# Attention and convolution kernel: first period reordered, x1 passed through DRAM in another layout, keys and values moved behind the transposes

## What is computed

```python
# per sequence b: a 32x32 mixing of the tokens, whose weights come from cond
h = gelu(gelu(cond @ W0 + b0) @ W1 + b1);  att = softmax(h @ W2 + b2)
y[b] = einsum('k,koi->oi', att[b], weight) @ x[b] + (att[b] @ bias_k)[:, None]
# attention over the 32 tokens: 32 query heads, 8 key/value heads of 16, rope, causal
x1 = x + softmax(rope(y Wq) rope(y Wk).T / 4) (y Wv) @ Wo
# grouped convolution over the 512 channels (tokens are its channels): 4 groups, 9 taps
z = conv(x1) + cond @ c_weight.T + bias
# feed forward: base matrix and 8 LoRA experts, weighed by a router's softmax
out = x1 + z @ base_W.T + base_b + 2 * sum_e w_e * (z A_e.T) B_e.T
```

## Time and profile before

| | |
|---|---|
| median of 3 runs | 609.29 (609.05 to 610.1) |
| the profiled execution: its own time | 612.12 |
| the profiled execution: span of its instructions | 610.3 |
| PE busy | 586.5, 96% of the span |
| DVE / ACT / POOL busy | 494.5 / 221.4 / 225.9 |
| mean granted TensorE clock | 0.992 |

### The profile page before, as it was taken

One profiled execution on the slowest core, in us unless ns is written; L12 is line 12 of the kernel. 1 busy time (PEld: TensorE's weight loads), 2 busy tenths in 40 slices (PEclk: granted clock), 3 DMA queues, 4 the chain that ended last, 5 costly groups with the idle time before them and its releaser, 6 DMA issues.

```text
span 610.3 us, 14252 instructions
## 1 busy us (share of the span) xinstructions
PE 586.5 (96%) x4937; PEld 493.8 (81%) x4937; DVE 494.5 (81%) x1236; ACT 221.4 (36%) x603; POOL 225.9 (37%) x182
## 2 busy tenths in 40 slices
PE   5789999999999999999999999999999999999986
PEld 4577888888889888888888888888888888898864
DVE  4658788888888888888888888888888888888855
ACT  4344333333333333334333433333333334334321
POOL 7344244333333433233344333343443333334310
PEclk9879999999999999999999999999999999999999
DMA  8547553445555434455553345455534455554241
GB/s 186 109 145 158 117 130 107 94 113 112 116 133 133 116 96 111 99 112 133 133 133 109 90 111 111 113 133 133 129 101 97 107 117 117 133 133 112 64 112 59
DMA packets 122086, 71.26 MB, mean 117 GB/s; under 512 B 45661, under 2 KB 104189, under 8 KB 121944
## 3 DMA queue, kind: packets, MB, share of 16 engines
q1 hardware_dynamic: 120576, 70.53, 48.7%
q0 software_dynamic: 144, 0.28, 0.3%
q10 hardware_dynamic: 1352, 0.27, 0.2%
HBM read 51.53 MB, written 19.53 MB: 116 GB/s over the span
## 4 chain that ended last, share of the span: by engine, by line
PE 78%; DMA 10%; DVE 5%; SPq 3%; issue 2%; ACT 1%; ACTq 1%; DVEq 0%
PE ps L435 17%; PE ps L602 15%; PE ps L623 9%; DMA scratch<-x_dram 6%; PE ps L629 5%; PE ps L665 5%; PE ps L539 4%; PE ps L657 4%; PE ps L684 3%; PE ps L706 3%; PE ps L576 3%; PE ps L673 2%; PE ps L613 2%; PE ps L579 2%; DVE x1p L1290 1%
## 5 line engine op out<-in xcount | busy, mean ns | idle before, releaser
L1013 POOL TENSOR_TENSOR qk<-network,t 128x640 f32<-128x640 f32 x31 | 48.3, 1558 | 162.6 <-DVE t L1206 162.6
L435 PE MATMUL ps<-wqkv_hi,y_hi 128*128 128x512 f32 (+1 forms) x256 | 87.8, 343 | 0.9 <-POOL y_lo L1003 0.5
L435 PE MATMUL ps<-wqkv_lo,y_hi 128*128 128x512 f32 (+1 forms) x256 | 87.4, 342 | 0.0
L435 PE MATMUL ps<-wqkv_hi,y_lo 128*128 128x512 f32 (+1 forms) x256 | 87.4, 342 | 0.0
L1025 POOL TENSOR_TENSOR raw<-x1p,basebB 128x512 f32<-128x512 f32 x32 | 49.5, 1547 | 57.8 <-DVE x1p L1290 57.6
L799 ACT ACTIVATE raw<-ps 128x512 f32<-128x512 f32 x64 | 37.7, 595 | 76.0 <-PE ps L684 75.9
L1020 POOL TENSOR_TENSOR raw<-raw,zero 128x512 f32<-128x512 f32 x32 | 33.3, 1040 | 73.9 <-DVE raw L1279 73.9
L435 PEld LDWEIGHTS ps<-wqkv_hi,y_hi 128*128 128x128 f32 x256 | 48.8, 191 | 8.8 <-ACT y_hi L799 2.0
L997 POOL TENSOR_TENSOR raw<-raw,rz 128x512 f32<-128x512 f32 x32 | 33.6, 1049 | 59.4 <-DVE rz L1235 59.4
L435 PEld LDWEIGHTS ps<-wqkv_lo,y_hi 128*128 128x128 f32 x256 | 48.9, 191 | 6.1
L435 PEld LDWEIGHTS ps<-wqkv_hi,y_lo 128*128 128x128 f32 x256 | 48.8, 191 | 6.0
(11 more groups left out here) (204 smaller groups left out, 1468.9 us busy)
## 6 DMA issues: line engine op xcount, KB each, us to landing
scratch<-x_dram SPq DMA_DIRECT2D x96, 256.0 KB, 5.8
x_dram<-x1p SPq DMA_DIRECT2D x32, 260.0 KB, 2.0
xm<-x SPq DMA_DIRECT2D x32, 256.0 KB, 4.4
xr<-x SPq DMA_DIRECT2D x32, 256.0 KB, 2.7
out<-raw SPq DMA_DIRECT2D x32, 256.0 KB, 2.1
v_dram<-vS SPq DMA_DIRECT2D x32, 64.0 KB
vB<-v_dram SPq DMA_DIRECT2D x128, 16.0 KB, 4.8
mixb<-mixb_dram SPq DMA_DIRECT2D x28, 64.0 KB, 3.9
```

The source lines that it names most:

```text
L435: last = mm(dst, a, b, start=(n == 0), stop=(n == 3 * len(left) - 1))
L1013: nc.gpsimd.tensor_tensor(qk[:, :], t1, t2[:, :], ALU.add).then_inc(qk_sb, 1)
```

## The change

In the loop and the other periods:

- x1 is stored to DRAM by four DMAs (one for each phase j, each 128 runs of 520 bytes) in a layout in which each of the three xc loads is 32 runs of 8312 bytes; xc has rows of 130 columns in SBUF. All waits on `x1_out` count four DMAs.
- In t = 3 to 30 keys_values(t+1) stands behind transpose_p(t) on PE; in the others it stays.
- values' waits for vB and pT_sb become `values_ready`, which stands ahead of conv (in t = 1 behind it). The wait for `hwT_lo_sb` and the two-column product go. The hwT transpose goes to bank 3 in place of 7 (but for the last three groups).
- ACT copies both halves of the transposed probabilities before the transposed hw.

In the first period:

- SP, and not ACT, issues the loads of the mixing weights of groups 1 to 3, behind the broadcast of the bias and ahead of the store of v.
- PE runs scores(0) before it waits for these weights and mixes group 1. DVE runs the first half of softmax(0) ahead of the next y, the second half behind it.
- ACT copies v and q first, then Wo's first two parts, the exponentials' first half, and after the second half Wo's other two parts.

```diff
@@ -199,7 +199,8 @@
         oT_lo = sb("oT_lo", [P, NQ, NB, S], F32R)
         x1p = sb("x1p", [P, PH, P + 2])
         x1 = x1p[:, :, 1:P + 1]
-        xc = scratch[0:SHIFTS * S, 0:NB * PH * P].rearrange("p (q n) -> p q n", n=P)
+        xcs = scratch[0:SHIFTS * S, 0:NB * PH * (P + 2)]
+        xc = xcs.rearrange("p (q n) -> p q n", n=P + 2)[:, :, 0:P]
         z_hi = sb("z_hi", [P, PH, P], F32R)
         z_lo = sb("z_lo", [P, PH, P], F32R)
         arS = sb("arS", [P, NAR])
@@ -219,7 +220,7 @@
 
         mixb_dram = nc.dram_tensor("mixb_dram", [B, S], F32, kind="Internal").ap()
         v_dram = nc.dram_tensor("v_dram", [P, P], F32, kind="Internal").ap()
-        x1_dram = nc.dram_tensor("x1_dram", [NB * PH, CG * PH, P + 2], F32, kind="Internal").ap()
+        x1_dram = nc.dram_tensor("x1_dram", [CG * PH, NB * PH, P + 2], F32, kind="Internal").ap()
         mixw_dram = nc.dram_tensor("mixw_dram", [B, S, S], F32, kind="Internal").ap()
 
         bank = [ctx.enter_context(nc.psum_tensor(f"bank{i}", [P, 512], F32)) for i in range(0)]
@@ -300,6 +301,14 @@
         def heads(w, a):
 
             return w[:, :, :, :].rearrange("p g (b a) q -> p a g b q", a=2)[:, a, :, :, :]
+
+        def hwT_bank(u):
+
+            return 7 if isinstance(u, int) and u >= G - 3 else 3
+
+        def keys_late(t):
+
+            return not isinstance(t, int) or 3 <= t < G - 1
 
         def value_bank(a, t):
 
@@ -358,6 +367,9 @@
                     sp.dma_start(vB[S * k:S * (k + 1), :, :, at:at + HD].rearrange("m b h d -> m (b h) d"),
                                  v_dram.rearrange("(m b) (h k d) -> k m (b h) d", b=NB, h=2, d=HD)[k]).then_inc(vB_in, 16)
 
+            sp.wait_ge(mixw_zero, 1)
+            sp.wait_ge(mixw_out1, 16)
+            load_mixw(sp, 1, 4, mixw_in2)
             sp.wait_ge(pads_sb, 1)
             store_values(0)
             load_values(0)
@@ -389,10 +401,11 @@
                 if peeled(t, G - 1):
                     load_values(t)
                 if live(t - 1):
-                    sp.wait_ge(x1_out, 16 * t)
+                    sp.wait_ge(x1_out, 16 * PH * t)
+                    run = NB * PH * (P + 2) - 2
                     for s in range(SHIFTS):
-                        sp.dma_start(xc[S * s:S * (s + 1), :, :],
-                                     x1_dram[:, :, s:s + P].rearrange("q r n -> r q n")).then_inc(xc_in, 16)
+                        sp.dma_start(xcs[S * s:S * (s + 1), 0:run],
+                                     x1_dram.rearrange("r q n -> r (q n)")[:, s:s + run]).then_inc(xc_in, 16)
                 if live(t) and not peeled(t, 0) and not peeled(t, G - 1):
                     load_values(t)
                 if peeled(t, 1):
@@ -408,7 +421,8 @@
                     store_values(t + 1)
                 if live(t):
                     sp.wait_ge(x1_sb, t + 1)
-                    sp.dma_start(x1_dram.rearrange("q (i j) n -> (q i) j n", j=PH), x1p[:, :, :]).then_inc(x1_out, 16)
+                    for j in range(PH):
+                        sp.dma_start(x1_dram.rearrange("(i j) q n -> j q i n", j=PH)[j], x1p[:, j, :]).then_inc(x1_out, 16)
                 if live(t) and live(t + 1):
                     sp.dma_start(xr[:, :], group(x_g, t + 1)).then_inc(xr_in, 16)
                 if live(t + 3) and (not isinstance(t, int) or t > 0):
@@ -686,18 +700,17 @@
                     if b % 2:
                         last.then_inc(pT_ps, 1)
 
+            def values_ready(t):
+
+                pe.wait_ge(vB_in, 16 * HK * (t + 1))
+                pe.wait_ge(pT_sb, 2 * t + 2)
+
             def values(t):
 
-                pe.wait_ge(vB_in, 16 * HK * (t + 1))
-                if live(t - 2) and not peeled(t, G - 1):
-                    pe.wait_ge(hwT_lo_sb, t - 1)
                 if peeled(t, 0):
                     pe.wait_ge(prep_sb, 1)
                 if peeled(t, 1):
                     pe.wait_ge(base_lo_sb, 3)
-                pe.wait_ge(pT_sb, 2 * t + 2)
-                if not isinstance(t, int):
-                    mm(ps[0:S, 4, 0:2], convW[:, 0, :, :].rearrange("p j o -> p (j o)"), xc[:, 0, 0:2], start=True, stop=True)
                 for b in range(NB):
                     for h in range(2):
                         for r in range(2):
@@ -710,7 +723,7 @@
             def transpose_hw(u):
 
                 pe.wait_ge(hw_sb, u + 1)
-                nc.tensor.transpose(ps[:, 7, 0:P], hw[:, :, :].rearrange("p e r -> p (e r)"), ident).then_inc(hwT_ps, 1)
+                nc.tensor.transpose(ps[:, hwT_bank(u), 0:P], hw[:, :, :].rearrange("p e r -> p (e r)"), ident).then_inc(hwT_ps, 1)
 
             def steps(t):
                 if live(t):
@@ -726,6 +739,7 @@
                 if peeled(t, 3):
                     pe.wait_ge(mixw_in, 16 * NB)
                 if peeled(t, 0):
+                    scores(t)
                     pe.wait_ge(mixw_in2, 16 * NB)
                 if live(t + 1):
                     mix(t + 1)
@@ -734,7 +748,7 @@
                     mixing_weights()
                 if peeled(t, 2):
                     prepare_lora()
-                if live(t):
+                if live(t) and not peeled(t, 0):
                     scores(t)
                 if peeled(t, 0):
                     prepare_ar()
@@ -746,6 +760,7 @@
                     last_feed_forward()
                 if live(t + 1):
                     queries(t + 1)
+                if live(t + 1) and not keys_late(t):
                     keys_values(t + 1)
 
                 if peeled(t, -1):
@@ -757,7 +772,10 @@
                     keep_warm(6)
                 if live(t):
                     transpose_p(t)
+                if live(t + 1) and keys_late(t):
+                    keys_values(t + 1)
                 if peeled(t, G - 1):
+                    values_ready(t)
                     values(t)
                 if peeled(t, G):
                     keep_warm(4)
@@ -767,8 +785,13 @@
                 if peeled(t, G + 1):
                     keep_warm(2)
                     last_lora()
+                if live(t) and not peeled(t, G - 1):
+                    if not peeled(t, 1):
+                        values_ready(t)
                 if live(t - 1) and not peeled(t, G):
                     conv(t - 1)
+                if peeled(t, 1):
+                    values_ready(t)
                 if live(t) and not peeled(t, G - 1):
                     values(t)
                 if peeled(t, 1):
@@ -832,9 +855,6 @@
                 act.wait_ge(aggw_act, 1)
                 act.wait_ge(aggw_dve, 1)
                 act.dma_start(mixw_dram[NB:4 * NB, :, :], aggS[NB:4 * NB, :, :]).then_inc(mixw_out1, 16)
-                act.wait_ge(mixw_zero, 1)
-                act.wait_ge(mixw_out1, 16)
-                load_mixw(act, 1, 4, mixw_in2)
 
             def prepare_wo(heads):
                 act.wait_ge(ld["wo"], 16 * NKV)
@@ -883,7 +903,7 @@
             def high_hwT(t):
 
                 act.wait_ge(hwT_ps, t - 1)
-                copy(hwT_hi[:, :], ps[:, 7, 0:P]).then_inc(hwT_hi_sb, 1)
+                copy(hwT_hi[:, :], ps[:, hwT_bank(t - 2), 0:P]).then_inc(hwT_hi_sb, 1)
 
             def next_y_hi(u):
 
@@ -897,21 +917,21 @@
                 if live(t):
                     act.wait_ge(qT_ps, t + 1)
                     copy(qT, ps[:, 4, :].rearrange("p (g b q) -> p b g q", g=NQ, b=NB)).then_inc(qT_sb, 1)
+                if peeled(t, 0):
+                    prepare_wo((0, 1))
+                    exponentials(t, 0)
                 if live(t - 2):
                     act.wait_ge(zT_ps, t - 1)
                     copy(z_hi[:, :, :].rearrange("p j (q o) -> p j q o", o=CG), z_transposed(t - 2)).then_inc(z_hi_sb, 1)
                 if live(t + 1):
                     next_y_hi(t + 1)
-                if peeled(t, 0):
-                    prepare_wo((2, 3))
                 if peeled(t, -1):
                     keep_mixing_weights()
                     prepare_kv()
                     pass_mixing_weights()
-                    prepare_wo((0, 1))
                 if peeled(t, 2):
                     prepare_lora()
-                if live(t):
+                if live(t) and not peeled(t, 0):
                     exponentials(t, 0)
                 if live(t - 2):
                     act.wait_ge(ar_ps, t - 1)
@@ -919,6 +939,8 @@
                     copy(arS[:, :], ps[:, 7, at:at + NAR]).then_inc(ar_sb, 1)
                 if live(t):
                     exponentials(t, 1)
+                if peeled(t, 0):
+                    prepare_wo((2, 3))
                 if live(t - 2):
                     act.wait_ge(top_sb, t - 1)
                     nc.scalar.activation(ex[:, :], lg[:, :], ACT.Exp, bias=top[:, :], accum_out=exZ[:, :]).then_inc(ex_sb, 1)
@@ -929,12 +951,10 @@
 
                 if live(t):
                     transposed_p(t, 0)
-                if live(t) and peeled(t, G - 1):
+                if live(t):
                     transposed_p(t, 1)
```

(16 more changed lines are left out.)

## The result

The change makes the kernel slower: 782.94 us median (770.94 to 799.82, 4 runs) against 609.32 for the kernel before in the same session. Forecast were 601.0 and a range of 597 to 608.5. It is rival C, at nearly five times the loss that its main figure gave (+35). The profiled execution took 776.51, with a span of 774.7; that of before took 612.12.

The account below looks back on a forecast made before the run. PE was taken as the bound, with work in flight in 586.5 of 610.3 us. Terms -4.2 - 4.3 + 0.3 - 0.2 + 0.1 = -8.3, from the median 609.3, gave 601.0; range 597 to 608.5.

Parts of the forecast that it names:

- rival C: In each loop period vB lands after PE reaches its wait ahead of conv: slower, +35 (644); chance 0.15.
- The loop, what comes: Loop costs: three more stores on SP's queue, +1.3 of issues a period, yet vB and xc land without a wait.
- the landing of vB: In the loop, vB's last load, issued at 160.5, lands about 2.6 later, at 163.1: no wait, margin 0.2.
- The landing of xc: In the loop, xc's last load, issued at 157.9, has 5.4 until 163.3; alone in the old form it took 4.51.
- The added issues: Three more store DMAs on SP's queue ahead of xc and vB, 0.4 to 0.5 each: +1.3 a period.
- one way into C: The four stores run one after the other, 2.04 each, xc issued 4.4 later: 714; 0.02 of rival C's 0.15.
- The loop, what goes: In 27 loop periods, dropping the two-column product saves 0.16 each, -4.3; conv to the next piece stays 0.99.
- the other branch, up to 7.5: In the loop, without a drain between tiles, conv to the next piece shortens by some 0.12: up to 7.5 saved.
- First period: Before the loop: scores hidden under the weights' loads, queries 2.7 earlier, 1.5 more from a clock that stays up: -4.2.
- Periods 1, 2 and 32: Outside the loop: +0.3 for later vB, -0.2 for hw's wait gone, +0.1 for store and xc.

Follow-up runs that it names:

- warm kernel: Against the whole change: in loop periods, 16 products whose result nobody reads put ahead of the waits for vB and the probabilities; 730.63 us, ratio 1.194.
- the order alone: Against the kernel before: only PE's and ACT's new loop order, waits ahead of conv, no two-column product; old DMAs and first period; 621.98 us, ratio 1.022.

## Why the prediction was wrong

**The step that failed is in "The loop, what comes": the landing of vB.** The prediction put it at 2.6 behind the issue, on the ground that 1536 short runs become 96 long ones and the backlog shrinks. It was 5.8. The bytes are the same, and the runs of 8312 bytes landed later than any shorter ones of the four lengths tried. With the long runs and one store vB's median landing is 4.8, what it was before; with short runs and four stores it is 5.5, with both 5.7. So the long runs did not shrink the backlog, and what makes 5.8 of 4.4 stays open. The backlog is also more than the runs of xc: the prediction never counted xm's 256 KB, whose load moved behind brings vB's median from 5.7 to 4.8 and 58 us. But xm stood at the same place in the kernel before, 4.0 us ahead of the last issue of vB, where it is 3.9 now:

```profile
155.20 0.34 SPq L388 DMA_DIRECT2D xm<-x  x1
```

So it is part of the 4.4, and not what made it 5.8. The 2.0 to 2.5 of the earlier trace rows were no bound for this place: there vB stands ahead of xc.

**The landing of xc** failed beside it. The prediction gave its last load 5.4 us and set against that the 4.51 of period 32, where it goes alone. In the loop of the kernel before, the same load took 6.3, which from an issue at 157.9 is 164.2, already 0.9 late; after the change it took 7.7. Conv would have waited with vB on time, as the 77.0 us of the kernel with the wait behind conv show.

**The added issues** were the term +1.3; from the store to the last vB issue it was 2.1 more. Each of the four stores takes 0.56 to 0.60 on the queue, where the one that they replace took 0.34; I had 0.4 to 0.5. Together with the landing, vB came 3.8 late where I had it 0.2 early. The four did not run one after the other, which was one way into C: each landed after 2.2 in the median, from its own issue.

**Rival C's price** was linear, 2.7 us for each 0.1. For 3.8 late it gives 601 + 103 = 704, where 774 was measured. It left out that PE, standing for 3.9 us, works at a clock of 0.50 soon after it comes back: 1.6 more in each period, which the warm kernel's 43 us confirm. With these 43, the 16 of periods 1 to 3 and the 4 that the first period did not give, it is 767. The earlier trace rows had both the gap of 2.2 and the low clock behind it, and I used them for the first period alone. The chance of 0.15 rested on a margin of 0.2 under a term whose own bounds were 2.0 and 4.4 (a landing of 4.4 gave 1.6 late); with such bounds C should have had the larger chance.

**The loop, what goes** was right in size and half right in cause. The 0.16 goes (17.56 to 17.40), and conv to the next piece stays at 0.99 to 1.00 with nothing awaited behind it; the other branch, up to 7.5, is out. The rows of the kernel with the waits behind conv tell more: the two-column product, which has conv's own tile, starts 0.88 behind conv, and values, with another tile, 1.01, product or not (1.00 without it). So 0.12 more passes here before a product of another tile. The Trainium skill (TensorEngine Tiling (Array Packing), Key Properties) says that a change of tiling mode drains the TensorE, and these rows agree with it, though they don't show the drain itself. But the 0.16 was ACT's late copy: with keys, values and ACT's copies moved, 0.15 of it goes with the product still there.

**First period**: -4.2 was forecast, and nothing that can be told was measured. Two things failed. The chain of the kernel after shows what I had at nothing:

```profile
26.49 1.02 ACT wo_hi L822
...
27.58 3.03 POOL wo_lo L1008 x2
...
30.64 1.28 POOL y_lo L1023
...
32.06 6.00 PE ps L449 x24
```

ACT's copies of Wo now come behind q, POOL makes their low parts of them, and y's low part stands behind these 3.03 on POOL. The queries do start at 32.06, near the forecast (31.65), but from 32 to 38 the mean granted clock is 0.72, behind a gap of PE, and with the keys and values they take 6.00. And the execution that I set it against was one of the longer ones: in it the store of the mixing weights landed after 6.21. In the kernel with the order alone, whose first period is that of before, it landed after 4.32 and the queries started at 31.06 and took 4.41. The store before, then the order alone:

```profile
17.41 6.21 DMA mixw_dram<-scratch
```

```profile
17.42 4.32 DMA mixw_dram<-scratch
...
31.06 4.41 PE ps L443 x24
```

Period 0 of the unchanged code took 16.2, 17.5, 17.8, 21.3, 21.8 (the one of the prediction) and 23.3 in six profiled executions. The changed one takes 18.7 to 18.9: steadier, longer than three of these and shorter than three.

**Periods 1, 2 and 32**: the forecast was +0.2 in sum. Periods 1 to 3 took 16 more, for the same waits as in the loop.

## What to carry to other kernels

Before a wait is moved ahead of work that covers it, work out for the transfer it waits for all the data issued in the microseconds ahead of it on that queue, whoever wants it, and move what isn't urgent behind it: here one such move turned a loss of 12 us into a gain of 6. Take its landing from the rows of the loop, not from a place where it goes alone. Where a landing is known only within 2 us and the margin is 0.2, the bounds decide and not the middle, and the price of being late includes the clock that PE comes back with. A saving at one place that occurs once in a program should be set against several executions, not against the one that happened to be profiled.

## What the runs showed of the hardware

- A DMA of 779 KB in 96 rows whose source has 3 as its slowest dimension kept a DMA share of 0.19, that of 3 of the 16 engines, and the last load of vB behind it landed after 15.87 us.
- A store of 260 KB landed after 4.16 in runs of 520 bytes in a transposed order and after 2.04 in runs of 2080.
- Runs of 8312 bytes into 32 partitions landed no sooner than sixteen times as many of 512: 6.5 and 5.8 in the median, though three loads of the latter took 1.9 to issue and of the former 1.3.
- An issue on SP cost 0.34 for one store, and 0.56 to 0.60 for each of four to the transposed layout.
- Behind conv a product of the same tile started after 0.88, one of another tile after 1.00 to 1.01, with nothing awaited.
- After a stay of 3.9 us PE's granted clock was still 1.00 when work began and fell to 0.50 about 1 us later, for some 3 us.
